# Householder steps of an eigensolver: row b from an early column and a TensorE transpose, B in two tiles

## The reference

```python
def _L0_gnn_ref(features, A, W1, b1, W2, b2):
    deg = jnp.sum(A, axis=0) + jnp.sum(A, axis=1) - jnp.diagonal(A)
    d_inv_sqrt = jnp.where(deg > 0, jax.lax.rsqrt(deg), 0.0)
    L = jnp.diag(deg) - A
    L_norm = d_inv_sqrt[:, None] * L * d_inv_sqrt[None, :]
    _, U = jnp.linalg.eigh(L_norm)
    agg = jnp.einsum('mn,bnd->bmd', U.T, features)
    h = jax.nn.relu(agg @ W1 + b1)
    out = h @ W2 + b2
    return jnp.einsum('nm,bmd->bnd', U, out)
...
h = jnp.maximum(_layernorm(x, axis=-1), 0.0)
x = x + _L0_gnn_ref(h, adj, L0_gnn_W1, L0_gnn_b1, L0_gnn_W2, L0_gnn_b2)
h = jnp.maximum(_layernorm(x, axis=-1), 0.0)
x = x + _L1_gnn_ref(h, adj, ...)
h = jnp.maximum(_layernorm(x, axis=-1), 0.0)
x = x + _L2_gnn_ref(h, adj, ...)
h = jnp.maximum(_layernorm(x, axis=-1), 0.0)
x = x + _L3_gnn_ref(h, L3_gnn_W, adj)
```

## Time and profile before

| what | value |
| --- | --- |
| runs | 1569.43, 1570.09, 1570.28 us; median 1570.09 us |
| profiled execution | 1570.16 us, of it the span from the first to the last instruction 1568.5 us |
| busy | TensorE 72%, VectorE 67%, ScalarE 44%, GpSimd 16% of the span |
| granted TensorE clock | 0.879 on average; full over the whole stretch of the Householder steps |
| chain that ended last | TensorE 50%, VectorE 35%, ScalarE 4%, issue 7% |
| Householder steps | 126 steps; their last instruction on B starts at 410.9 us |

### The profile page before, as it was taken

How to read it: one execution, slowest core, us unless ns; L and a number is a source line. 1 busy time by engine, 2 the same in 40 slices (tenths; PEclk the granted TensorE clock), 3 DMA queues, 4 the chain that set the end, 5 groups by cost and what they waited for, 6 DMA issues and landing times.

```text
span 1568.5 us, 21564 instructions
## 1 busy us (share of the span) xinstructions
PE 1124.1 (72%) x5260; PEld 714.5 (46%) x5260; DVE 1045.5 (67%) x4156; ACT 690.6 (44%) x1760; POOL 253.9 (16%) x900
## 2 busy tenths in 40 slices
PE   3777777776542300448787668999999998589998
PEld 2445555555421200335453356444455443367777
DVE  7777788777889999755576754444343354664766
ACT  2334444444231200024365457675554545365665
POOL 4045555666450000000000000000010020000000
PEclk9999999999975555559898679999999999597999
DMA  4000000000100000000000000000000000000001
GB/s 138 1 1 1 1 1 1 1 1 2 29 21 1 1 0 0 1 0 0 0 0 0 0 0 0 0 0 0 0 0 0 0 0 0 0 15 13 27 20 34
DMA packets 16654, 12.30 MB, mean 8 GB/s; under 512 B 665, under 2 KB 14530, under 8 KB 16578
## 3 DMA queue, kind: packets, MB, share of 16 engines
q1 hardware_dynamic: 16578, 11.49, 2.6%
HBM read 7.23 MB, written 4.19 MB: 7 GB/s over the span
## 4 chain that ended last, share of the span: by engine, by line
PE 50%; DVE 35%; issue 7%; ACT 4%; DVEq 1%; DMA 1%; POOL 1%; ACTq 0%; POOLq 0%
PE P L1343 30%; PE P L690 9%; PE P L1492 4%; DVE B L348 2%; DVE arena L330 2%; DVE arena L444 2%; DVE arena L495 1%; DVE arena L493 1%; DVE scal L320 1%; DVE bst_all L909 1%; ACT hb L1154 1%; DVE arena L448 1%; DVE arena L259 1%; DVE arena L337 1%; PE P L1485 1%
## 5 line engine op out<-in xcount | busy, mean ns | idle before, releaser
L1343 PE MATMUL P<-arena,WT 128*128 (+2 forms) x792 | 329.1, 579 | 3.9 <-ACT L1242 2.9
L1343 PEld LDWEIGHTS P<-arena,WT 128*128 128x128 f32 x792 | 151.8, 192 | 181.1 <-issue 167.3
L690 PE MATMUL P<-arena 1*128 1x127 f32 (+62 forms) x504 | 166.1, 434 | 87.1 <-DVE arena L330 48.6
L1255 ACT ACTIVATE arena<-P,bl 128x512 f32<-128x512 f32 (+1 forms) x252 | 153.3, 636 | 139.5 <-PE P L1343 130.7
L690 PEld LDWEIGHTS P<-arena 1*128 1x128 f32 x504 | 124.1, 307 | 142.4 <-DVE arena L330 112.8
L898 POOL COPY arena<-arena 128x512 f32<-128x512 f32 x16 | 21.5, 1386 | 783.0 <-DVE arena L1075 691.2
L1064 DVE TENSOR_TENSOR arena<-arena 128x512 f32<-128x512 f32 (+1 forms) x36 | 22.0, 610 | 137.4 <-ACT arena L1255 137.4
L652 ACT ACTIVATE arena<-arena 1x127 f32<-1x127 f32 (+62 forms) x126 | 32.2, 256 | 167.5 <-DVE arena L341 157.2
L1154 ACT ACTIVATE hb<-xN,nmr,rsd 128x128 f32 (+1 forms) x192 | 78.5, 481 | 34.9 <-PE P L1343 28.1
L690 PE MATMUL P<-arena,Ib 128*128 128x46 bf16 (+1 forms) x318 | 34.4, 268 | 60.9 <-ACT arena L679 60.4
L195 POOL TENSOR_SCALAR lf<-lf 1x1 f32<-1x1 f32 x210 | 73.3, 349 | 21.9
(11 more groups left out here) (477 smaller groups left out, 2451.2 us busy)
## 6 DMA issues: line engine op xcount, KB each, us to landing
out_dram<-xN SPq DMA_DIRECT2D x16, 256.0 KB, 2.3
Wn<-in_L_gnn_Wih_dram SPq DMA_DIRECT2D x4, 256.0 KB, 2.9
Wn<-in_L_gnn_Whh_dram SPq DMA_DIRECT2D x4, 256.0 KB, 2.8
Wqkv<-in_L_gnn_W_dram SPq DMA_DIRECT2D x1, 192.0 KB, 3.6
W1n<-in_L_gnn_W_dram SPq DMA_DIRECT2D x1, 128.0 KB, 4.1
W2n<-in_L_gnn_W_dram SPq DMA_DIRECT2D x1, 128.0 KB, 4.0
Wg<-in_L_gnn_Wg_dram SPq DMA_DIRECT2D x2, 64.0 KB, 3.6
adj<-in_adj_dram SPq DMA_DIRECT2D x1, 64.0 KB, 1.8
```

The costliest lines, as they stand in the source:

```text
L690: def mm(o,l,r,start=True,stop=True): return t.matmul(o,lhsT=l,rhs=r,start=start,stop=stop)
L1255: act(s.gt[u][gate][:,0:cols],P[4*u+gate][:,0:cols],f,bias=s.bl[:,4*(p-1)+gate:4*(p-1)+gate+1]).then_inc(ev('lstm_gates'),1)
L1343: def mm(o,l,r,start=True,stop=True,**k): return t.matmul(o,lhsT=l,rhs=r,start=start,stop=stop,**k)
```

## The change

VectorE adds one column of the new B first, into a tile of its own, `bcol`: old column k+2 plus column k+2 of P[3]. Then it adds all of B as before, but from one tile into the other (`Bk`, `B` and `B1`, in turn). TensorE makes row b of the next step by transposing `bcol` against the full identity, at the new semaphore `next_column`, in place of the matmul of an identity column with the whole of B. For step 0, VectorE copies column 1 of B to `bcol`. Since each of the two tiles now holds every other finished column, the two cuts of the diagonals read them with a stride of two: the first leaf place has four instructions for two, the last cut six for two.

```diff
--- before.py
+++ after.py
@@ -73,6 +73,8 @@
     tmp=sb("tmp",[N,N])
     B=sb("B",[N,N])
     xcol=sb("xcol",[N,1])
+    bcol=sb("bcol",[N,1])
+    Bk=[B,sb("B1",[N,N])]
     arena1=sb("arena1",[N,16384])
     arena2=sb("arena2",[N,8192])
     reflector_store=arena1[0:1,0:N*K]
@@ -304,6 +306,7 @@
         v.wait_ge(ev('reflectors_zeroed'),2)
         v.tensor_copy(reflector(0)[:,1:N],B[0:1,1:N]).then_inc(ev('x_row'),1)
         v.wait_ge(ev('x_row'),1)
+        v.tensor_copy(bcol[:,:],B[:,1:2]).then_inc(ev('next_column'),1)
         v.sem_inc(ev('B_updated'),1)
         def sign_of_x0(k):
             x0=reflector(k)[:,k+1:k+2]
@@ -345,13 +348,17 @@
             if k>=LEAF_FROM: leaf_at(2*(k-LEAF_FROM)+1)
             v.wait_ge(ev('B_updated'),k+1)
             v.wait_ge(ev('outer_products'),k+1)
-            tt(B[:,k+1:N],B[:,k+1:N],P[3][:,k+1:N],ALU.add).then_inc(ev('B_updated'),1)
+            old,new=Bk[k%2],Bk[(k+1)%2]
+            if k+1<K: tt(bcol[:,:],old[:,k+2:k+3],P[3][:,k+2:k+3],ALU.add).then_inc(ev('next_column'),1)
+            tt(new[:,k+1:N],old[:,k+1:N],P[3][:,k+1:N],ALU.add).then_inc(ev('B_updated'),1)
         def leaf_at(spot):
             sweep,phase=divmod(spot,SPOTS)
             if spot==0:
                 v.wait_ge(ev('B_updated'),LEAF_FROM+1)
-                c.mark(tt(wide[:,0:17],B[:,0:17],I[:,0:17],ALU.mult))
-                c(tt(wide[:,N:N+17],B[:,0:17],super_mask[:,0:17],ALU.mult))
+                for q in range(2):
+                    c.mark(tt(wide[:,q:17:2],Bk[q][:,q:17:2],I[:,q:17:2],ALU.mult))
+                    c.mark(tt(wide[:,N+q:N+17:2],Bk[q][:,q:17:2],super_mask[:,q:17:2],ALU.mult))
+                c.wait(c.n)
                 v.sem_inc(ev('tridiagonal_cut'),1)
             if spot==2:
                 v.wait_ge(ev('leaf_constants'),5)
@@ -387,8 +394,12 @@
         for k in range(K): hh_step(k)
         v.wait_ge(ev('B_updated'),K+1)
 
-        c(tt(wide[:,0:N],B[:,:],I[:,:],ALU.mult))
-        tt(wide[:,N:2*N],B[:,:],super_mask[:,:],ALU.mult).then_inc(ev('tridiagonal_cut'),1)
+        for q,first,end in ((0,0,K),(1,1,K),(K%2,K,N)):
+            step=2 if end==K else 1
+            c.mark(tt(wide[:,first:end:step],Bk[q][:,first:end:step],I[:,first:end:step],ALU.mult))
+            c.mark(tt(wide[:,N+first:N+end:step],Bk[q][:,first:end:step],super_mask[:,first:end:step],ALU.mult))
+        c.wait(c.n)
+        v.sem_inc(ev('tridiagonal_cut'),1)
         v.wait_ge(ev('tridiagonal_rows'),2)
         c(v.tensor_copy(diag[:,:],P[2][:,0:N]))
         c(v.tensor_copy(off[:,:],P[2][:,N:2*N]))
@@ -698,10 +709,11 @@
         def hh_step(k):
             t.wait_ge(ev('x_row'),k+1)
             mm(P[4][:,0:1],reflector(k),I[0:1,0:1]).then_inc(ev('column_psum'),1)
+            t.wait_ge(ev('next_column'),k+1)
+            t.transpose(P[0][0:1,0:N],bcol[:,:],I[:,:]).then_inc(ev('row_b_psum'),1)
             t.wait_ge(ev('B_updated'),k+1)
-            mm(P[0][0:1,k:N],I[:,k+1:k+2],B[:,k:N]).then_inc(ev('row_b_psum'),1)
             t.wait_ge(ev('column'),k+1)
-            mm(P[1][0:1,k:N],xcol[:,:],B[:,k:N]).then_inc(ev('row_xB'),1)
+            mm(P[1][0:1,k:N],xcol[:,:],Bk[k%2][:,k:N]).then_inc(ev('row_xB'),1)
             t.wait_ge(ev('Bv'),k+1)
             t.wait_ge(ev('v_scaled'),k+1)
             mm(P[3][:,k+1:N],Bv_row[:,:],v_row[:,k+1:N],stop=False)
```

## The result

The changed kernel takes 1581.68 us (median of 10 runs, 1570.07 to 1585.26) where the kernel before, on the same chip, takes 1569.43 (10 runs, 1567.34 to 1570.28): a ratio of 1.0063, 95% interval 1.0041 to 1.0085 (it goes by the means, 1578.85 and 1568.99 us; the ratio of the medians is 1.0078). It is slower, by 12 us in these medians and by 10 when both were timed again. I had forecast 1571.1, range 1566.0 to 1576.5. Ten runs of the change spread over 15 us, the ten of the kernel before over 3; that spread turns out to be the key. The profiled execution took 1579.53 us (before: 1570.16).

The account below looks back on a forecast made before the run. It took the order of waits inside one Householder step between TensorE and VectorE as the bound. Terms of -3.8, -1.3, +5.7 and +0.4 us gave +1.0 us on 1570.16: 1571.1 us, range 1566.0 to 1576.5.

Parts of the forecast that it names:

- from bcol's add to B's add: On VectorE, the small add delays the add of B and everything behind it by 0.08 us, bounds 0.07 to 0.15.
- transpose holds TensorE: One pass of 128 f32 columns occupies TensorE for 0.21 us per step, bounds 0.16 to 0.42.
- row b there: Row b, copied by ScalarE, is ready at z+0.64 in every step; z is the start of the step's first update add.
- x'B behind xcol, late: In late steps, x'B, now with two waits, starts 0.12 us behind xcol's end instead of 0.06.
- row Bv in steps 5, 45, 94: New VectorE start of L330: z+1.16, 1.07 and 0.97 to 0.98, against z+1.43, 1.12 and 0.91 before.
- steps 1 to 15, 16 to 47, 48 to 125: Householder steps gain 3.8 us early and 1.3 us in the middle, then lose 5.7 us late.
- ends: Copy ahead of step 0, two more leaf instructions and the six-piece last cut together add 0.4 us.
- the first term: Householder steps 1 to 15: gains from 0.30 down to 0.22 us per step, together -3.8 us.
- The slower rival in which the add costs its full length: The add of B starts only when bcol is written, 0.15 us: 6.7 us slower, about 1577 us; chance 0.20.
- the one with two passes: Slower rival: the transpose takes two passes on TensorE, about +9 us, 1579 us; chance 0.05.
- the faster rival: x'B's two waits cost nothing and the small add 0.06 us: 1566.4 us; chance 0.20.
- Behind the steps nothing is faster or slower; DMAs, the Sturm stage and the layers only shift.: After the Householder steps, later stages only shift in time, so the sum gives them no cost.

Follow-up runs that it names:

- experiment 8: The changed kernel with bcol added in every step but never read, row b from the matmul as before: one execution, 1574.47 us (kernel before 1568.81).
- the second profile: Profile of the changed kernel run again with no edit: 1568.69 us total, diagonal's copy at 415.71 us, attention 201.7 us.
- experiment 3: The kernel before with seven idle VectorE copies behind the last Householder step, nothing of the change in it: 1579.34 us, ratio 1.0055.
- experiment 2: The kernel before with the tiles bcol and B1 reserved but never used: 1569.09 us, ratio 0.9981.
- experiment 1: The changed kernel again with no edit: median 1579.34 us over 12 runs (1567.84 to 1584.19), ratio 1.0048 against the kernel before.
- experiment 5: early45 with 12 or 16 idle copies behind the last step, moving its cut back: 1557.34 us (ratio 0.9928) and 1556.77 us (ratio 0.9925).
- the best version: The changed kernel with bcol and transpose in steps 0 to 44 only and x'B's two waits swapped there: 1555.07 us, ratio 0.9913 against the kernel before.
- early45: The changed kernel with bcol and transpose in steps 0 to 44 only, row b by matmul from step 45: 1555.49 us, ratio 0.9902 against the kernel before.

## Why the prediction was wrong

**The steps, by its own terms.** Here it held in the main:

| term | predicted | measured |
| --- | --- | --- |
| from bcol's add to B's add | 0.08 us (0.07 to 0.15) | 0.07 to 0.08; 0.067 per step from experiment 8 |
| transpose starts | z+0.22 | z+0.21 to 0.22 |
| transpose holds TensorE | 0.21 us (0.16 to 0.42) | 0.30 |
| row b there | z+0.64 | z+0.59 |
| x'B behind xcol, late | 0.12 us | 0.14 |
| row Bv in steps 5, 45, 94 | z+1.16, 1.07, 0.97 to 0.98 | z+1.20, 1.08, 1.00 |
| distance in step 5 | 3.37 us | 3.41 |
| distance in step 118 | 2.56 us | 2.54 |
| steps 1 to 15, 16 to 47, 48 to 125 | -3.8, -1.3, +5.7 us | -2.8, -1.0, +6.0 |
| ends | +0.4 us | +0.2 |
| stage with its cut | +1.0 us | +2.3 (and +2.7 in the second profile) |

The term that was mis-sized is the transpose's hold on TensorE. I took a quarter of a run of four passes less the last one's own length, 0.21 us. The next matmul, which loads other weights, starts 0.30 us after it. So in the early steps the transpose and not xcol with its waits bounds x'B, at z+0.52 and not z+0.46. Since x'B is 0.02 us shorter than I took, row Bv comes 0.04 us late by this in step 5, and steps 2 to 15 gain 3.0 us where I had some 3.6. The other 0.4 us of the first term are step 1 alone, which loses 0.14 us where I had a gain of 0.30. The row x ahead of it starts late, before and after:

```profile
24.66 0.34 DVE L341 SCALAR_TENSOR_TENSOR arena<-arena 1x126 f32<-1x126 f32 x1
```

```profile
25.10 0.34 DVE L344 SCALAR_TENSOR_TENSOR arena<-arena 1x126 f32<-1x126 f32 x1 [0.54 <-DVE arena L340]
```

What that wait of 0.54 us is stays open; step 1 loses 0.14 us in the kernel of experiment 8 too, where nothing reads bcol, so it isn't the transpose. The slower rival in which the add costs its full length, the one with two passes (the row has one instruction of 128 columns, 0.37 us) and the faster rival all fell.

On the small add, the rows of before were right to be preferred. The Trainium skill (Perfetto Trace Analysis, Optimizing Scalar/DVE Operations) gives about 125 ns of access overhead for a VectorE operation on PSUM and says that profiled latency is about twice the engine-busy time. This case's add reads PSUM, and pushed everything behind it back by 0.067 us, so a sum by 0.125 for some 80 steps would have been an estimated 4.6 us too slow.

**The step that failed** is the sentence "Behind the steps nothing is faster or slower; DMAs, the Sturm stage and the layers only shift." It took a shift to be free of cost. The prediction itself had named as a sign of being wrong in its core that "the time moves outside the Householder stage", and that is what happened. Of the profiled 9.3 us, 2.3 are the stage's, 1.7 are given back between the cut and attention (952.0 us before, 950.3 after; without a delay in it this stretch takes 949.2 to 952.0 us over all profiles), and 8.7 are attention at a lower granted clock. Shown is: that attention's length goes with its time at half clock (the table of all profiles, one matmul taking 2.05 or 1.10 us, a turn of 27.7 or 22.9); that it happens without the change (experiment 3), and doesn't need it (experiment 2 has before's times, experiment 1 a run of the change with a shorter attention than before's); that added idle time alone moves the total by +10 or by -9 us. So the measured 10 us are real for this program, since its runs fall on the long patterns more often (15 of 22 at 1574.98 us or more; 3 of 102 of the kernel before, all three on one chip), but its steps are worth +2.3 us, and the rest is a side effect. That it comes by the shift, and not by something else that the changed steps do to the later stages, is argued from experiment 3, in which a shift of 1.8 us does the same; it isn't shown for the change itself.

The profile of before had the hint: two digits below eight at the right of its clock line, and the matmul of 2.05 us beside the one of 1.10. I had quoted "full over the whole stretch of the Householder steps" and left the other stages, since nothing in them was touched. With that seen, the sum would have been much the same, but the range would have had to reach some 10 us to both sides; mine held only the steps' uncertainty. The chance of 0.28 for slower was the steps' too.

The Trainium skill (TensorE: Matmul & The Clock Gate, Part 1) says that the gate's window runs freely and doesn't restart with the kernel, so that one kernel meets it differently from run to run. The two profiles of the change agree with that: 31.1 and 51.7 us at half clock in the same stage. The same part of the Trainium skill puts the penalty of the ramp to full clock at under 1% of a typical kernel's span; the falls here lie in the middle of a stage. Those two executions differ by 10.8 of 1580 us, 0.7%, and that is as large as all that was to be measured.

**What stays open** is what decides which pattern an execution takes. Not the time of the cut since the program's start (experiment 5: 413.0 in both, 12 us apart), not the start of attention (1362.61 and 1362.91 give 193.2 and 217.3 us), not the code behind the steps, which is the same in all. In the seventeen profiles, attention has 85 turns of the kind above, and in each there is one pair of idle pieces, 0.34 us and then a second one. The clock falls in 29 of them, each time 0.7 to 1.4 us behind the start of the matmul that the second piece stands ahead of. (Besides, it falls once near the end of the stage in every profile.) The second piece is 0.27 to 0.43 us long in 50 turns, 24 of them with a fall, and 0.16 to 0.20 us in 35, 5 of them with a fall. In the five profiles without such a fall it is always the short one, as in this timeline of the best version:

```profile
1415.07 1.05 PE L1509 MATMUL P<-arena 128*128 128x33 f32 x8 [0.34 <-ACT arena L1317]
1416.46 1.08 PE L1509 MATMUL P<-arena 128*128 128x33 f32 x8
...
1426.28 1.05 PE L1509 MATMUL P<-arena 128*128 128x33 f32 x8 [0.34 <-ACT arena L1317]
1427.97 1.08 PE L1509 MATMUL P<-arena 128*128 128x33 f32 x8 [0.17 <-ACT arena L1317]
...
1437.78 1.05 PE L1509 MATMUL P<-arena 128*128 128x33 f32 x8 [0.34 <-ACT arena L1317]
```

(here a turn takes 22.71 us). But the short piece doesn't keep the clock up by itself. In the long execution of early45 the clock falls at 1478.9 for 10.2 us, behind these rows:

```profile
1476.07 1.05 PE L1509 MATMUL P<-arena 128*128 128x33 f32 x8 [0.34 <-ACT arena L1317]
...
1477.76 1.08 PE L1509 MATMUL P<-arena 128*128 128x33 f32 x8 [0.17 <-ACT arena L1317]
```

So the place of the falls is shown, and the length of the idle piece does not decide alone. I didn't try to remove it, which would be the test. The rows ahead of the falls hold 16 transposes (L1485), but so do the turns without a fall, and no run here changed them. How much of early45's 13.6 us would last in other runs is open for the same reason. Its 4.3 us in the steps are shown, and with 3 and 4 us of idle time added it stayed at 1555.7 to 1561.3 us.

## What to carry to other kernels

Price a step where it stands in the loop, not for the loop: the same edit gained 0.23 us in a step with 123 columns and lost 0.09 in one with 34, and kept to the first 45 steps it is worth 4.3 us in the stage. Before a change of a few microseconds is believed, compare the stage that it touches (here to 0.4 us over two profiles), look at the granted clock of every stage in which TensorE is full, and run the kernel before with a little idle time in the place of the change: if that alone moves the total by more than the edit's own working, the total judges the clock and not the edit. Where a matmul waits for two semaphores, wait first for the one that comes last.

## What the runs showed of the hardware

- A transpose of 128 x 1 (one f32 instruction with 128 columns, 0.37 us in the row) holds TensorE for 0.30 us before a matmul with other weights starts (steps 2 to 12, in both orders of the waits).
- Of two waits ahead of a matmul, the late one costs 0.05 us when it is written first and 0.14 when it is written second (323.09 to 323.14, 324.61 to 324.75). The outer product's pair of the earlier trace rows has the same 0.14.
- A VectorE add of 128 x 1 that reads PSUM is 0.15 us long in the rows and delays what follows by 0.067.
- Half clock in a stage where TensorE is busy 92% of the time costs 4.9 us per stretch of 10.2; where VectorE is busy 27 of 30 us, 30.7 us of it cost nothing measurable. Some 3.4 us of useless work ahead made the kernel 9 us faster, 1.8 us made it 10 us slower.
